# First sum's stores and tap loads issued from GpSimd, VectorE's averages moved, rotation loads split

## The reference

```python
def reference(x, L0_conv_weight, L1_conv_rota_matrix):
    # depthwise 5x5 convolution, padding 2: 16 of the 25 taps are not zero,
    # eight are the weights 1..8 of a channel and eight their negatives
    x = x + conv(_gn(x), build_rpdc_kernel(L0_conv_weight), groups=128)
    # one 128x128 matrix per row h
    x = x + einsum('hvc,bchw->bvhw', rota_matrix, _gn(x))
    return x
```

## Time and profile before

| | us |
|---|---|
| median of 3 runs | 558.55 (557.21 to 558.85) |
| the profiled execution | 558.65 |
| its span in the trace | 556.8 |

### The profile page before, as it was taken

The page is one execution under the profiler, slowest core; times in us unless marked ns, Lnnn a source line. Parts: engine busy times, 40 slices in busy tenths (PEclk is TensorE's granted clock), DMA queues, the critical chain, the costliest instruction groups (busy, mean ns, idle before and its releaser), DMA issues.

```text
span 556.8 us, 8400 instructions
## 1 busy us (share of the span) xinstructions
PE 450.6 (81%) x3024; PEld 172.8 (31%) x3024; DVE 347.2 (62%) x649; ACT 361.4 (65%) x598; POOL 186.0 (33%) x299
## 2 busy tenths in 40 slices
PE   0169999999898898989899899962998778788772
PEld 0123333333333333333333233321443333333330
DVE  3426787877876876686778768561574544544533
ACT  1066887787777678768877888842675455455550
POOL 0223534433533533353344335301343233233230
PEclk9999999999999999899899999995899998998997
DMA  6898788989889888889988989937999999999999
GB/s 155 200 201 167 204 218 222 244 220 226 244 216 226 225 225 216 219 216 235 223 224 243 226 224 308 274 85 235 375 394 397 394 396 397 396 398 396 395 394 325
DMA packets 214329, 150.03 MB, mean 269 GB/s; under 512 B 138384, under 2 KB 179472, under 8 KB 214288
## 3 DMA queue, kind: packets, MB, share of 16 engines
q1 hardware_dynamic: 214288, 149.49, 92.0%
HBM read 82.14 MB, written 67.33 MB: 268 GB/s over the span
## 4 chain that ended last, share of the span: by engine, by line
SPq 30%; DMA 28%; DVE 13%; ACT 12%; PE 11%; issue 4%; DVEq 0%
SPq L165 23%; DMA out_dram<-area 21%; ACT area L305 8%; PE ps L434 7%; DMA area<-tap_lines 7%; DVE stats L382 3%; DVE area L365 3%; DVE area L414 3%; DVE stats L389 3%; SPq L179 2%; PE ps L482 2%; ACT area L294 2%; SPq L227 2%; ACT area L322 2%; SPq L172 1%
## 5 line engine op out<-in xcount | busy, mean ns | idle before, releaser
L434 PE MATMUL ps<-area 64*64 64x512 f32 x2560 | 297.8, 607 | 8.5 <-ACT area L322 8.5
L267 POOL TENSOR_SCALAR area<-area,affine 128x256 f32<-128x256 f32 x192 | 132.9, 707 | 222.1 <-DVE affine L375 222.1
L305 ACT ACTIVATE area<-ps 64x512 f32<-64x512 f32 x256 | 150.4, 587 | 10.6 <-PE ps L434 5.9
L482 PE MATMUL ps<-area 128*128 128x512 f32 x256 | 123.7, 630 | 34.9 <-ACT area L343 28.1
L434 PEld LDWEIGHTS ps<-area 64*64 64x64 f32 x2560 | 93.2, 134 | 158.5 <-issue 156.9
L414 DVE TENSOR_TENSOR area<-ps,area 128x512 f32<-128x512 f32 x128 | 81.2, 685 | 85.7 <-DMA out_dram<-area 68.6
L335 ACT ACTIVATE area<-area,norm 128x256 f32<-128x256 f32 x160 | 82.1, 588 | 72.2 <-DMA area<-x_scratch 58.5
L365 DVE TENSOR_TENSOR area<-area 128x1024 f32<-128x1024 f32 x64 | 78.8, 1232 | 77.1 <-ACT area L305 77.0
L294 ACT ACTIVATE area<-area 64x1280 f32<-64x1280 f32 x64 | 81.3, 1270 | 60.1 <-DMA area<-tap_lines 59.2
L279 POOL TENSOR_SCALAR area<-area,norm 128x256 f32<-128x256 f32 x96 | 52.0, 555 | 132.9 <-DMA area<-x_scratch 81.0
L389 DVE BATCH_NORM_STATS2 stats<-area 128x6 f32<-128x512 f32 x128 | 79.9, 685 | 10.8 <-DMA area<-in_x_dram 10.8
(11 more groups left out here) (22 smaller groups left out, 38.3 us busy)
## 6 DMA issues: line engine op xcount, KB each, us to landing
area<-in_x_dram SPq DMA_DIRECT2D x256, 128.0 KB, 3.3
x_scratch<-area SPq DMA_DIRECT2D x64, 512.0 KB, 6.0
area<-x_scratch SPq DMA_DIRECT2D x32, 1024.0 KB, 12.4
out_dram<-area SPq DMA_DIRECT2D x32, 1024.0 KB, 11.3
area<-tap_lines SPq DMA_DIRECT2D x32, 330.0 KB, 5.1
tap_lines<-line SPq DMA_DIRECT2D x1, 200.0 KB, 3.1
norm_scratch<-affine SPq DMA_DIRECT2D x8, 2.0 KB
rot_all<-_L_conv_rota_matrix_dram SPq DMA_DIRECT2D x4, 0.5 KB, 10.4
```

The lines of the kernel that those rows point to most:

```text
L267: last = nc.gpsimd.tensor_scalar(padded[k % GRING][:, :, j, PAD:PAD + W], xin[k % XRING][:, j], affine[:, k, 0, 0, j:j + 1], affine[:, k, ...
L305: last = nc.scalar.activation(y[k % YRING][rows, 2 * pair + c], ps[half, bank + n].rearrange("p (j w) -> p j w", j=J), ACT.Identity)
L434: last = nc.tensor.matmul(ps[half, bank + n], taps[k % 2][rows, 2 * pair + c, d], padded[k % GRING][rows, 2 * pair + c, :, d:d + W], start ...
L482: nc.tensor.matmul(ps[:, m % 6, :], rot_t[u % 2][:, h], gn[n % NRING][:, h], start=True, stop=True).then_inc(rotated, 1)
```

## The change

Stores of the sums, the store of the tap lines and the loads of the taps are issued in the Pool's program. SyncE keeps the x loads, the norms, the rotations and the whole second stage. In the Pool's step s stand now the stores of group s-2 and the taps of group s+1, ahead of the normalisation of group s+1.

VectorE takes the averages of round s+2 ahead of the x statistics of group s+3.

The granule slots are 7 in place of 6 and permuted. The first five granules are loaded in two parts: the channels of the first 28 groups, when these are stored, and the remaining 16 channels when all are.

```diff
-IRING = 6
+IRING = 7
+EARLY = 5
+EARLY_SLOTS = (4, 5, 6, 0, 1, 2, 3)
+EARLY_GROUPS = 28
...
-        tin = [piece((RH, J, W)) for _ in range(IRING)]
+        slots = [piece((RH, J, W)) for _ in range(IRING)]
+        tin = [slots[n] for n in EARLY_SLOTS]
...
+        def granule_landings(n):
+            return 16 * (n // IRING + 1) + (16 if n % IRING < EARLY else 0)
...
-            for k in range(2):
-                load(k)
-            sp.wait_ge(line_ready, len(POS_IDX + NEG_IDX))
-            sp.dma_start(tap_lines, line[:]).then_inc(line_stored, 16)
-            load(2)
-            load(3)
-            sp.wait_ge(line_stored, 16)
-            load_taps(0)
-            load_taps(1)
-            for k in range(4, XRING - 1):
+            for k in range(XRING - 1):
                 load(k)
 
             for s in range(GROUPS + 3):
                 if group(s + XRING - 2) and s >= 1:
                     if s >= 2:
                         sp.wait_ge(x1_ready, 2 * (s - 1))
                     load(s + XRING - 2)
-                if group(s + 2):
-                    sp.wait_ge(taps_ready, 2 * (s + 1))
-                    load_taps(s + 2)
-                if group(s - 1):
-                    sp.wait_ge(x1_ready, 2 * s)
-                    store(s - 1)
                 if group(s - 3) and (s - 2) % NBATCH == 0:
                     store_norms(s - 2 - NBATCH)
...
-            for n in range(YRING):
-                sp.wait_ge(x1_stored[n], 32 * (GROUPS // YRING))
...
+            early, late = slice(0, EARLY_GROUPS * GC), slice(EARLY_GROUPS * GC, C)
+            for k in range(YRING):
+                sp.wait_ge(x1_stored[k], 32 * (EARLY_GROUPS // YRING))
+            for n in range(EARLY):
+                sp.wait_ge(x1_ready, 2 * (XRING * ((GROUPS - 1 - EARLY_SLOTS[n]) // XRING) + EARLY_SLOTS[n] + 1))
+                load_granule(n, early).then_inc(in_landed[n], 16)
+            for k in range(YRING):
+                sp.wait_ge(x1_stored[k], 32 * (GROUPS // YRING))
...
-            load_granule(0)
+            for n in range(EARLY):
+                load_granule(n, late).then_inc(in_landed[n], 16)
             sp.wait_ge(norm2_stored, 32 * (GROUPS // NBATCH))
             sp.dma_start(norm2[:], norm2_dram).then_inc(norm2_landed, 16)
-            for n in range(1, IRING):
-                load_granule(n)
+            for n in range(EARLY, IRING):
+                load_granule(n, slice(0, C)).then_inc(in_landed[n], 16)
...
+            pool.wait_ge(line_ready, len(POS_IDX + NEG_IDX))
+            pool.dma_start(tap_lines, line[:]).then_inc(line_stored, 16)
+            pool.wait_ge(line_stored, 16)
+            load_taps(0)
+            load_taps(1)
+
             for s in STEPS:
+                if group(s - 2):
+                    pool.wait_ge(x1_ready, 2 * (s - 1))
+                    store(s - 2)
+                if group(s + 1) and s >= 1:
+                    pool.wait_ge(taps_ready, 2 * s)
+                    load_taps(s + 1)
                 k = s + 1
                 if group(k):
                     pool.wait_ge(affine_ready, k + 1)
```

More of the change, by code:

```diff
@@ L167, in load @@
                                      ).then_inc(x_landed[slot], 16)
[L169 to L180, removed]
             def store_norms(first):
@@ L218, in _, with load_granule @@
                     sp.dma_start(rot_all[:, rows], rota_src[:, rows]).then_inc(rot_landed, 16)
-            for n in range(YRING):
-                sp.wait_ge(x1_stored[n], 32 * (GROUPS // YRING))
-            def load_granule(n):
+            def load_granule(n, channels):
                 u, half = n // 2, n % 2
[L225 to L229, removed]
+                return sp.dma_start(tin[n % IRING][channels].rearrange("p h j w -> p h (j w)"),
+                                    x1_dram[channels, u * RH:(u + 1) * RH, half * J:(half + 1) * J, :].rearrange(
+                                        "c h j w -> c h (j w)"))
+            early, late = slice(0, EARLY_GROUPS * GC), slice(EARLY_GROUPS * GC, C)
[6 more added lines that the diff above has]
+                sp.wait_ge(x1_stored[k], 32 * (GROUPS // YRING))
             def store_granule(n):
@@ L244, in _ @@
                 if n + IRING < GRANULES:
-                    load_granule(n + IRING)
+                    load_granule(n + IRING, slice(0, C)).then_inc(in_landed[(n + IRING) % IRING], 16)
             for n in range(ORING):
@@ L258, in _, with load_taps, store @@
                                     pattern=[[-1, P]], channel_multiplier=1).then_inc(ident_ready, 1)
-            for s in STEPS:
+            def load_taps(k):
+                window = bass.AP(tensor=tap_lines.tensor, offset=k * GC * LINE,
+                                 ap=[[1, H], [LINE, GC], [1, WINDOW]])
+                pool.dma_start(taps_raw[k % 2][0:H].rearrange("p c d h -> p c (d h)"), window
+                             ).then_inc(taps_landed[k % 2], 16)
+            def store(k):
+                for n in range(2):
+                    rows = slice(n * HALF, (n + 1) * HALF)
+                    dst = x1_dram[k * GC:(k + 1) * GC, :, n * J:(n + 1) * J, :].rearrange("c h j w -> h c (j w)")
+                    pool.dma_start(dst, y[k % YRING][rows].rearrange("p c j w -> p c (j w)")
+                                 ).then_inc(x1_stored[k % YRING], 16)
+            pool.wait_ge(line_ready, len(POS_IDX + NEG_IDX))
[3 more added lines that the diff above has]
+            load_taps(1)
+            for s in STEPS:
+                if group(s - 2):
[4 more added lines that the diff above has]
+                    load_taps(s + 1)
                 k = s + 1
@@ L274, in _ @@
             for n in range(GRANULES):
-                pool.wait_ge(in_landed[n % IRING], 16 * (n // IRING + 1))
+                pool.wait_ge(in_landed[n % IRING], granule_landings(n))
                 if n >= NRING:
@@ L330, in _ @@
             for n in range(GRANULES):
-                act.wait_ge(in_landed[n % IRING], 16 * (n // IRING + 1))
+                act.wait_ge(in_landed[n % IRING], granule_landings(n))
                 if n >= NRING:
@@ L384, in _ @@
                             in_=y[(s - 1) % YRING][:, :, 2 * q:2 * q + 2].rearrange("p c j w -> p c w j"))
[L385 to L393, removed]
                 if is_round(s + 2):
@@ L405, in _ @@
                                                    ).then_inc(spread_ready, 1)
+                if group(s + 3):
+                    k = s + 3
+                    dve.wait_ge(x_landed[k % XRING], 16 * 2 * GC * (k // XRING + 1))
+                    for q in range(J // 2):
+                        last = nc.vector.bn_stats(
+                            out=stats[:, k % 2, 0, 2 * q:2 * q + 2].rearrange("p j f -> p (j f)"),
+                            in_=xin[k % XRING][:, 2 * q:2 * q + 2].rearrange("p j c w -> p (c w) j"))
+                if is_round(s + 3):
+                    last.then_inc(stats_ready, 1)
                 if group(s):
```

## The result

The changed kernel took 575.8 us (572.9 to 577.5) against 558.7 (557.2 to 561.3) of before: ratio 1.0295, 95% interval 1.0234 to 1.0356. It is slower, where I had forecast 535.3 and a range of 522 to 565. All these are medians of four runs, with the lowest and the highest. The profiled execution took 572.86 with a span of 571.1.

The account below looks back on a forecast made before the run. SyncE's issuing of x loads, stores and taps was taken as the bound. Group 1 at 34.0, plus 307.8 for 31 groups, minus 0.3, plus 11.3, 180.6 and 1.85, gave 535.3 us, range 522 to 565.

Parts of the forecast that it names:

- rival B: Steady groups: TensorE is the bound throughout, 31 groups at 9.62 us, time 526; chance 0.20.
- Start: Before the steady groups: tap lines stored at once by the Pool, conv 0 at 21.5, group 1 at 34.0, 11.2 us earlier.
- c: Pool's time to issue one store or taps load: taken as 1.2 us, between bounds 0.62 and 2.18.
- A: Steady groups: the Pool's queue becomes the bound, slower, time 567 at an issue of 2.18 us; chance 0.22.
- L: Steady groups: time of a taps load from issue to landing, taken as 6.0 us, the median behind two stores.
- my own loop: Two-group loop: 11.9 us from taps landed through normalisation, two store issues 2.4, taps landing 6.0; 20.3, or 10.15 each.
- The free groups: Steady groups: ScalarE can take taps 3.5 us late before TensorE stands, so some 7 groups run at 9.62.
- the last six: End of the steady groups: no x loads beside the last six groups, so they run at 9.62 us each.
- SyncE's rest: Steady groups: x loads keep 0.68 us an issue, 5.4 a group, leaving SyncE's queue idle some 4 us a group.
- The boundary: Last affine to end: norms' read behind five granules instead of one, 180.6 us in place of 175.7, 4.9 more.
- The averages: VectorE's averages ahead of x statistics: variance matmul input 2.5 us earlier, removing TensorE's 1.7 us wait; why the floor is 9.62.
- rival C: Steady groups: transfers, not issues, set the 10.48 us; only start and boundary change, time 552; chance 0.11.

Follow-up runs that it names:

- e11: e5 with the stores of the sum put back on SyncE behind the x loads of a step; 541.6 us, ratio 0.972 to the kernel before.
- e5: Changed kernel with taps issued ahead of the stores on the Pool, and whole granules with the norms' read behind one; 524.1 us, ratio 0.940 to before.
- e1: Changed kernel with one edit: the Pool issues the taps load ahead of the two stores of the sum; 542.2 us, ratio 0.972 to the kernel before.
- e10: e6 with the taps of group 1 loaded behind the normalisation of group 0; 518.4 us, ratio 0.931 to the kernel before.
- e6: e1 with the early parts issued ahead of the last norms store and the norms' read right behind that store; 521.4 us, ratio 0.935 to before.
- e3: Changed kernel with whole granules loaded at the boundary, the norms' read behind five of them; 566.5 us, ratio 1.015 to the kernel before.
- e9: e1 with granules split by rows, each part 128 channels by two rows; 532.1 us, ratio 0.955 to the kernel before.
- e7: e1 with granule parts of 64 and 64 channels in place of 112 and 16; 543.3 us, ratio 0.974 to the kernel before.

## Why the prediction was wrong, point by point

- **What bounds the kernel before: right.** e11 and e5 show it from both sides: with only the taps off SyncE its issues still fill more than TensorE's 9.62 a group, and with stores and taps off it TensorE is the bound. e1 and e5 run the 31 groups at the 9.62 of rival B.
- **Start: right in kind, 2.3 us short.** The term "0.6 for x loads that share the engines with taps" measured 3.8 (x of group 1 at 18.48), and the first convolution started at 24.76, not 21.5. e10 gave part of it back.
- **The Pool's issue, c: 0.65, not 1.2.** A whole rival (A, the Pool as the bound) hung on 2.18. It lost its cause, yet the time came out on its side: it was to decide from 331 us for the 31 groups, and they took 330.9. That is the rival's luck, not its mechanism. (By its own terms its sum is 339.4, not 339.6, and 331 is reached at a c of 1.97, not 1.85.)
- **The step that failed: L.** I took 6.0, the landing of the stores, for a load that stands behind two of them in one queue; it measured 8.4. Put into my own loop this gives 11.9 + 1.3 + 8.4 = 21.6, the turn measured above, 10.8 a group, where I had 20.3; the smaller c gave back 1.1 of the 2.4. e1 shows that the taps' place decides: with the taps ahead of the stores they land in 5.7 us, and TensorE is at its floor. The rule of the sum (2c + L ≤ 7.3 for the floor) holds on both sides: 1.3 + 8.4 is above it, and in e1 the stores' issues are no longer in the loop.
- **The free groups: wrong.** By the starts of the variance matmuls, TensorE stayed at 9.62 a group for 4 groups after the start (35.95 to 74.42), not 7; 21 groups at 10.81 followed, and the last six took 10.90 each, where I had 9.62. Of the 23.1 us missed in the groups, about 12 are the rate, 4 the free groups and 8 the last six. The reserve of 3.5 was worked out with one of the two evictions (2.42 each) that ScalarE has in a group, so it had no sound source. The rule for the last six, that nothing slows them once the x loads are over, passed over the rotations: their four loads, no longer spread out by what stood between them in SyncE's queue, were issued at once from 308.89, and one taps load took 12.3 us. That they are the cause is not shown. Before, with the four loads spread out, one taps load took 11.6; in e1 they are issued at once too and no group is slower.
- **SyncE's rest: wrong, without weight.** The issues of the x loads became longer, 1.23 in place of 0.68, and SyncE was never idle for 4 us a group.
- **"The early loads are not early": right,** and e6 shows what the name was worth, 2.7 us beside e5.
- **The boundary: mis-sized.** The queue's part was 6.9 us (I had 4.9). I priced the parts at 397 GB/s, the rate of whole granules; they moved 266 and 109. That term was missing, 9.6 us. I had no row with a granule load on fewer than 128 partitions and never asked whether 112 would run like 128.
- **The averages: right as the reason why 9.62 is the floor.** They are worth 0.3% by themselves and 8.3 us with the rest mended. The wait for the spread goes whichever way the taps come, as I wrote, but with late taps TensorE waits as long for something else.
- **Transfers as the bound (rival C): no.** The share went to 1.03, but e1 moved 255 GB/s of the same loads.
- **What two queues gain.** The Trainium skill says in "DMA: Bandwidth & Descriptors", section Issuing engines are not separate DMA queues, that issuing from several engines saves only the sequencer's time, usually small beside the transfer. Between e11 and e5 the stores' two issues alone leave SyncE, 1.29 us a group, and N comes 18.0 us sooner. So the trace does not agree that the time is small here, where eight x loads of 128 KB a group fill the queue. The whole step from 558.2 to 524.1 is more than issue time: it holds the start (7.8 us of span sooner) and up to 8.3 us that hang on the averages.

The sum of the misses in span: start 2.3, groups 23.1, boundary 12.4, in all 37.8, and 533.4 + 37.8 = 571.2 against 571.1.

## What to carry to other kernels

When transfers move to another queue, write down the order inside the new queue and what it makes wait: the small load that an engine needs next goes ahead of the big store that nobody waits for. A landing time read from the old queue belongs to the old place in it; for the new place add up what stands ahead. And a load that is cut by partitions is priced at its own rate, not at that of the whole one.

## What the runs showed of the hardware that was not expected

- Loads from DRAM into SBUF in pieces of 2 KB moved about 390 GB/s on 128 partitions (e3, e9), 245 to 268 in parts of 112 (e1, changed kernel), 206 to 226 on 64 (e7) and 109 to 129 where parts of 16 were last (changed kernel, e1), each with a DMA share of 1.04 to 1.12. The share says that engines are occupied, not how many bytes move.
- A DMA of 256 pieces issued from GpSimd took 0.65 us of its time, about as much as SyncE's 0.63. It is shown as a queue of its own (software_dynamic).
- Two queues together moved 255 to 257 GB/s at a share of 0.96 to 1.01 (e1, 100 to 300 us) in a mix in which one queue had moved 225 at 0.88; and with the second queue at work SyncE's issue of an x load went from 0.64 us to 0.85 in the median (changed kernel).
